# Attention kernel: values and sums of two key tiles in one visit every second step, maxima transposed by VectorE, score banks four and two

## What is computed

```
ada = silu(c) @ Wada + bada
shift_msa, scale_msa, gate_msa, shift_mlp, scale_mlp, gate_mlp = split(ada, 6)
h = _ln(x) * (1 + scale_msa) + shift_msa
q, k, v = (h @ W + b).reshape(B, L, H, DH) for each of the three
A = softmax(scale * einsum('blhe,bshe->bhls', q, k))
out = einsum('bhls,bshd->blhd', A, v)
x = x + gate_msa * (out @ Wo + bo)
m = gelu((_ln(x) * (1 + scale_mlp) + shift_mlp) @ W1 + b1) @ W2 + b2
return x + gate_mlp * m
```

## Time and profile before

| | us |
|---|---|
| median of 3 runs | 2636.14 |
| lowest and highest | 2632.66, 2636.88 |
| span of the profiled execution | 2625.2 |
| of it: up to the first score of head 0 | about 358 |
| heads 0 to 31 | about 358 to 2178 |
| stage 3 | the rest |
| PE busy | 2543.3 (97%) |
| DVE busy | 1841.4 (70%) |
| POOL busy | 1625.0 (62%) |
| ACT busy | 1309.9 (50%) |

### The profile page before, as it was taken

One profiled execution on the slowest core, in us unless ns is written; L12 is line 12 of the kernel. 1 busy time (PEld: TensorE's weight loads), 2 busy tenths in 40 slices (PEclk: granted clock), 3 DMA queues, 4 the chain that ended last, 5 costly groups with the idle time before them and its releaser, 6 DMA issues.

```text
span 2625.2 us, 45742 instructions
## 1 busy us (share of the span) xinstructions
PE 2543.3 (97%) x13208; PEld 1482.7 (56%) x13208; DVE 1841.4 (70%) x2872; ACT 1309.9 (50%) x2429; POOL 1625.0 (62%) x744
## 2 busy tenths in 40 slices
PE   7999899999999999999999999999999979999998
PEld 5788654444444444444444444444444437888887
DVE  5444588887877878778777787778778745555553
ACT  3333245665666656666666665666656642222221
POOL 0000157887888878888878888878888772112120
PEclk9999999999999999999999999999999989999999
DMA  7655631111211112211122111122111001121100
GB/s 263 207 192 167 153 112 49 33 34 39 60 34 33 33 38 56 40 33 33 35 44 56 33 33 35 35 52 46 33 34 33 21 25 53 49 73 71 48 32 32
DMA packets 141459, 163.15 MB, mean 62 GB/s; under 512 B 76048, under 2 KB 92944, under 8 KB 134032
## 3 DMA queue, kind: packets, MB, share of 16 engines
q1 hardware_dynamic: 140480, 159.95, 23.2%
q10 hardware_dynamic: 720, 0.02, 0.0%
HBM read 100.95 MB, written 58.72 MB: 61 GB/s over the span
## 4 chain that ended last, share of the span: by engine, by line
PE 93%; DVE 3%; issue 1%; ACT 1%; DMA 1%; SPq 0%; POOL 0%; ACTq 0%; POOLq 0%; DVEq 0%
PE ps L1113 21%; PE ps L1015 20%; PE ps L1104 19%; PE ps L1127 18%; PE ps L1118 7%; PE ps L1248 7%; DVE part_max L868 1%; PE ps L1024 1%; DVE weights_r L882 1%; PE ps L1059 1%; PE ps L1047 0%; DMA work<-v_rows 0%; DVE work L942 0%; ACT work L670 0%; DMA work<-in_x 0%
## 5 line engine op out<-in xcount | busy, mean ns | idle before, releaser
L538 POOL TENSOR_TENSOR work<-work 128x1024 f32<-128x1024 f32 x640 | 1505.7, 2395 | 296.7 <-PE ps L1118 262.7
L868 DVE TENSOR_REDUCE part_max<-ps 128x1 f32<-128x512 f32 x1984 | 1229.0, 682 | 321.3 <-PE ps L1104 320.7
L670 ACT ACTIVATE work<-ps 128x512 f32<-128x512 f32 x2048 | 1070.9, 602 | 697.3 <-PE ps L1113 697.2
L1113 PE MATMUL ps<-acts_r 97*128 97x512 f32 x2048 | 836.4, 418 | 26.0 <-ACT work L670 14.7
L1104 PE MATMUL ps<-acts_r 96*128 96x512 f32 x1984 | 811.3, 409 | 6.8 <-DVE part_max L868 6.7
L1113 PEld LDWEIGHTS ps<-acts_r 97*128 97x128 f32 x2048 | 383.1, 190 | 396.7 <-ACT work L670 308.4
L1127 PE MATMUL ps<-work 128*32 128x512 f32 x4096 | 545.3, 604 | 0.0
L1104 PEld LDWEIGHTS ps<-acts_r 96*128 96x128 f32 x1984 | 375.6, 189 | 263.0 <-DVE part_max L868 182.4
L1015 PE MATMUL ps<-acts_r,weights_r 128*128 128x512 f32 x1536 | 380.3, 397 | 5.7 <-DVE acts_r L790 5.7
L1015 PEld LDWEIGHTS ps<-acts_r,weights_r 128*128 128x128 f32 x1536 | 291.1, 191 | 69.3 <-issue 6.8
L547 POOL TENSOR_TENSOR work<-work,gate_b 128x512 f32<-128x512 f32 x60 | 84.5, 1439 | 214.3 <-DMA work<-in_x 172.8
(11 more groups left out here) (69 smaller groups left out, 897.5 us busy)
## 6 DMA issues: line engine op xcount, KB each, us to landing
work<-in_x SPq DMA_DIRECT2D x16, 1024.0 KB, 5.4
acts_r<-q_hi SPq DMA_DIRECT2D x64, 256.0 KB, 4.8
acts_r<-k_hi SPq DMA_DIRECT2D x64, 256.0 KB, 6.4
q_hi<-work SPq DMA_DIRECT2D x32, 256.0 KB, 2.6
q_lo<-work SPq DMA_DIRECT2D x32, 256.0 KB, 3.3
k_hi<-work SPq DMA_DIRECT2D x32, 256.0 KB, 2.6
k_lo<-work SPq DMA_DIRECT2D x32, 256.0 KB, 3.2
v_rows<-work SPq DMA_DIRECT2D x32, 256.0 KB, 2.0
```

The lines of the kernel that those rows point to most:

```text
L538: nc.gpsimd.tensor_tensor(psum_acc[:, at], first, prob[:, t % RING, at], ALU.add).then_inc(add_ok, 1)
L670: nc.scalar.activation(prob[:, t % RING, j * CH:(j + 1) * CH], ps[:, A_BANKS + (u + t * NQ + j) % B_BANKS, :], ACT.Exp, scale=SCALE).then_ ...
L868: nc.vector.tensor_reduce(part_max[:, f // NQ, f % NQ:f % NQ + 1], ps[:, (u + f) % A_BANKS, :], AX.X, ALU.max).then_inc(a_max, 1)
L1113: nc.tensor.matmul(ps[:, A_BANKS + (u + t * NQ + j) % B_BANKS, :], ks[u][0:M_ROW + 1, t * P:(t + 1) * P], qs[u][0:M_ROW + 1, j * CH:(j + 1 ...
```

## The change

Six edits, all in stage 2.

1. The groups no longer stand in each step. `BREAKS` puts those of tiles 0, 1 and 2 in step 3, and from step 5 on those of `t-2` and `t-1` in every odd step, each tile's sum behind its values (`use_tile`). Step 1 takes the last tile of the head before and its closing sum. The groups of a head remain 22.
2. The maximum is not transposed by TensorE. `row_max` is widened to 32 columns, VectorE transposes it in blocks of 32x32 into `max_T`, and the row of q is written by four DMAs of 16x32 elements.
3. It is not negated: the row of k holds -1 in the place of 1.
4. PSUM: four banks for the max pass, two for scores.
5. ScalarE takes output and denominators of the head before both after step 1.
6. GpSimd adds tile 13 in the place of 11, TensorE sums 11 in the place of 13. Two slots of the ring change names for stage 3, so that `norm_apply` waits for tile 14 in the place of 13.

```diff
-POOL_TILES = [0, 1, 2, 3, 5, 6, 7, 9, 10, 11, 12]
+POOL_TILES = [0, 1, 2, 3, 5, 6, 7, 9, 10, 12, 13]
...
-STEP_MAX = NT - 2
-A_BANKS, B_BANKS = 3, 3
+BREAKS = {3: (0, 1, 2), **{t: (t - 2, t - 1) for t in range(5, NT, 2)}}
+STEP_LAST = 1
+A_BANKS, B_BANKS = 4, 2
...
+MAX_PIECES = 4
...
-        SLOT_XC1, SLOT_XN3, SLOT_OTF, SLOT_HTF3 = range(RING)
+        SLOT_XC1, SLOT_OTF, SLOT_XN3, SLOT_HTF3 = range(RING)
...
-        row_max = sb("row_max", [P, NT])
-        neg_max = sb("neg_max", [NT, P], F32R)
+        row_max = sb("row_max", [P, DH])
+        max_T = sb("max_T", [P, DH])
...
-                sp.wait_ge(neg_ok, g + 1)
-                sp.dma_start(qs[u][M_ROW:M_ROW + 1, :].bitcast(F32),
-                             neg_max[:].bitcast(F32)).then_inc(neg_in, 16)
+                sp.wait_ge(maxT_ok, g + 1)
+                row = qs[u][M_ROW:M_ROW + 1, :].bitcast(F32).rearrange("o (t q) -> o t q", q=P)
+                for w in range(MAX_PIECES):
+                    sp.dma_start(row[:, :, w * DH:(w + 1) * DH], max_T[w * DH:w * DH + NT, :]).then_inc(maxT_in, 16)
...
-            def row_of_ones(u):
-                nc.gpsimd.memset(ks[u][M_ROW:M_ROW + 1, :].bitcast(F32), 1.0).then_inc(ones_row, 1)
-                pool.wait_ge(ones_row, u + 1)
-            row_of_ones(0)
+            def row_of_minus_ones(u):
+                nc.gpsimd.memset(ks[u][M_ROW:M_ROW + 1, :].bitcast(F32), -1.0).then_inc(minus_row, 1)
+                pool.wait_ge(minus_row, u + 1)
+            row_of_minus_ones(0)
...
-                        nc.scalar.activation(prob[:, t % RING, j * CH:(j + 1) * CH], ps[:, A_BANKS + (u + t * NQ + j) % B_BANKS, :],
+                        nc.scalar.activation(prob[:, t % RING, j * CH:(j + 1) * CH], ps[:, A_BANKS + (t * NQ + j) % B_BANKS, :],
                                              ACT.Exp, scale=SCALE).then_inc(exp_ok, 1)
-                    if prev and t == 0:
+                    if prev and t == STEP_LAST:
                         take_output(g - 1, (u + 2) % NBUF, uses)
-                    if prev and t == 1:
                         take_denominator(g - 1)
...
-                nc.vector.tensor_reduce(row_max[:], part_max[:], AX.X, ALU.max).then_inc(max_ok, 1)
-            def negate_max(g):
-                dve.wait_ge(maxT_mm, g + 1)
                 if not isinstance(g, int) or g:
-                    dve.wait_ge(neg_in, g * 16)
-                nc.vector.tensor_scalar(neg_max[:], ps[0:NT, 0, 0:P], -1.0, None, ALU.mult).then_inc(neg_ok, 1)
+                    dve.wait_ge(maxT_ok, g)
+                else:
+                    dve.wait_ge(zero_ok, 1)
+                nc.vector.tensor_reduce(row_max[:, 0:NT], part_max[:], AX.X, ALU.max).then_inc(max_ok, 1)
+            def transpose_max(g):
+                dve.wait_ge(max_ok, g + 1)
+                if not isinstance(g, int) or g:
+                    dve.wait_ge(maxT_in, g * (16 * MAX_PIECES))
+                nc.vector.transpose(max_T[:], row_max[:]).then_inc(maxT_ok, 1)
...
-                    nc.vector.tensor_reduce(part_max[:, f // NQ, f % NQ:f % NQ + 1], ps[:, (u + f) % A_BANKS, :], AX.X, ALU.max).then_inc(a_max, 1)
+                    nc.vector.tensor_reduce(part_max[:, f // NQ, f % NQ:f % NQ + 1], ps[:, f % A_BANKS, :], AX.X, ALU.max).then_inc(a_max, 1)
                 row_maxima(g)
-                negate_max(g)
+                transpose_max(g)
...
-            def transpose_max(g):
-                pe.wait_ge(max_ok, g + 1)
-                nc.tensor.matmul(ps[0:NT, 0, 0:P], row_max[:], ident[:], start=True, stop=True).then_inc(maxT_mm, 1)
...
-            chunk(NCHUNK - 1, 1, nxt=False, max_after=FILLS_7, max_at=MAX_AT_7)
+            chunk(NCHUNK - 1, 1, nxt=False, max_after=FILLS_7)
             assert next(fills, None) is None
             def max_scores(g, u, f):
                 pe.wait_ge(a_max, g * FILLS + f - A_BANKS + 1)
                 j = f % NQ
-                nc.tensor.matmul(ps[:, (u + f) % A_BANKS, :], qs[u][0:M_ROW, f // NQ * P:(f // NQ + 1) * P],
+                nc.tensor.matmul(ps[:, f % A_BANKS, :], qs[u][0:M_ROW, f // NQ * P:(f // NQ + 1) * P],
                                  ks[u][0:M_ROW, j * CH:(j + 1) * CH], start=True, stop=True).then_inc(a_mm, 1)
             def scores(g, u, t, j):
                 if t == 0 and j == 0:
-                    pe.wait_ge(neg_in, g * 16 + 16)
+                    pe.wait_ge(maxT_in, (g + 1) * (16 * MAX_PIECES))
                 if not isinstance(g, int) or g or t or j >= B_BANKS:
                     pe.wait_ge(exp_ok, START + g * (NT * NQ) + t * NQ + j - B_BANKS + 1)
-                nc.tensor.matmul(ps[:, A_BANKS + (u + t * NQ + j) % B_BANKS, :], ks[u][0:M_ROW + 1, t * P:(t + 1) * P],
+                nc.tensor.matmul(ps[:, A_BANKS + (t * NQ + j) % B_BANKS, :], ks[u][0:M_ROW + 1, t * P:(t + 1) * P],
...
-            def last_values(g, u):
-                values(g, u, NT - 1)
-                if NT - 1 in PE_TILES:
-                    tile_sum(g, NT - 1)
+            def use_tile(g, u, t):
+                values(g, u, t)
+                if t in PE_TILES:
+                    tile_sum(g, t)
...
-                    pe.wait_ge(neg_ok, g + 1)
...
-                    if t == 0 and prev:
-                        last_values(g - 1, (u + 2) % NBUF)
-                    if t == 1 and prev:
+                    if t == STEP_LAST and prev:
+                        use_tile(g - 1, (u + 2) % NBUF, NT - 1)
                         finish_denominators(g - 1)
-                    if t >= 2 and t - 2 in PE_TILES:
-                        tile_sum(g, t - 2)
-                    if t >= 1:
-                        values(g, u, t - 1)
+                    for tile in BREAKS.get(t, ()):
+                        use_tile(g, u, tile)
...
-                    if nxt and t == STEP_MAX:
-                        transpose_max(g + 1)
                 assert next(fills, None) is None
-                if NT - 2 in PE_TILES:
-                    tile_sum(g, NT - 2)
-            pe.wait_ge(ones_row, 1)
+            pe.wait_ge(minus_row, 1)
             pe.wait_ge(v_ok, START + NCHUNK * TT)
             head(0, 0, 1, False, True)
-            pe.wait_ge(ones_row, NBUF)
+            pe.wait_ge(minus_row, NBUF)
```

19 lines of the change are left out of this document (9 added, 10 removed).

## The result

| us | before | after |
|---|---|---|
| median of the runs | 2635.78 | 2783.35 |
| lowest and highest | 2632.66, 2636.88 | 2777.63, 2792.85 |
| ratio, 95% interval | | 1.0572 [1.0547, 1.0598] |
| span of the profiled execution | 2625.2 | 2775.8 |
| up to head 0's first score | 357.5 | 358.05 |

The change makes the kernel 5.5 to 6.0% slower, as forecast in kind, 46 us above the forecast of 2737. That lies inside the range of 2665 to 2795, but above the 2765 that the forecast's own errors were to reach; the range held it because it was drawn to take in rival B, the falling clock.

What follows compares the result with a forecast made beforehand. TensorE was taken to bound looped heads. 30 x 3.45 = 103.5, -7 at loop turns and +4.5 in the last head gave +101 on the span of 2625.2, 2726; with 10.9 to the median, 2737, range 2665 to 2795.

Steps and rivals of the forecast that it cites:

- rival B: TensorE's clock falls in waits around head ends: about 2790 with one fall each head, 2753 each third head; chance 0.11.
- The looped head: Heads 1 to 30: waits for score banks add 7.0 us, breaks and transpose save 3.57, so 3.45 more each.
- the turn of a bank: Two scores in the same PSUM bank start at least 1.19 us apart; four products between them take only 0.94.
- the quarter in each step: First score of steps 1 to 14 comes 0.25 us late for its bank, 3.5 a head.
- The transpose: Dropping TensorE's transpose of the maxima saves 0.51 us in each looped head.
- The reorder window: Skill's rule, not followed: weight loads pulled ahead make some 20 late scores about 0.1 less late, total about 2677.
- The turn of the loop: Every third head: instructions arrive while the first score waits 0.72 for its bank, 10 x 0.7 = 7 us back.
- the row of maxima: Transpose and four DMAs land 4.3 us behind the row maximum (4.1 to 5.15), hidden before the next head's first score.
- Head 0: First head, held by VectorE, whose work is unchanged: 0, between -3 and +3 us.
- The last head and stage 3: Waits in the last head and norm_apply's later start add 4.5 us, between 0 and +8; stage 3 untouched.
- Rival C: The four DMAs of maxima land one after the other, first score 2.8 us late: +84, 2820; chance 0.05.
- Rival A: Score banks don't bind, a turn under 0.98 between max products: faster, 2530 to 2615; chance 0.12.

Runs made afterwards that it cites:

- experiment 4: Changed kernel with both ScalarE copies moved from behind step 1 to behind step 2: 2758.41 us.
- experiment 1: Kernel before with one edit, four banks for the max pass and two for scores: 2763.56 us.
- experiment 2: Changed kernel with three banks for the max pass and three for scores again: 2728.62 us.
- experiment 5: Kernel before with edits 2 and 3 alone (maxima transposed by VectorE, four DMAs, -1 in the row of k): 2636.07 us, ratio 1.0002.
- experiment 6: Changed kernel with the previous head's last-tile groups and closing sum in step 0, both ScalarE copies behind step 2: 2733.09 us.
- experiment 3: Changed kernel with exponentials of heads 1 to 30 over 256 of 512 columns: 2674.43 us.
- experiment 9: Changed kernel with TensorE's loop unrolled to six heads a turn: 2791.72 us.
- 10: Changed kernel with the loops of TensorE and ScalarE unrolled to 15 heads a turn: 2753.40 us, ratio to before 1.0452.
- 11: Changed kernel with three banks each, groups merged only in steps 5, 9, 12 and 15, max products redistributed, last tile in step 0: 2603.24 us, ratio 0.9874.
- 12: Kernel of experiment 11 with TensorE's loop at six heads a turn: 2598.73 us, ratio 0.9864.

## Why the prediction was right or wrong

**The looped head: right.** Forecast 58.6, which is 3.45 more than before; measured 58.73, 3.63 more. Over 30 heads the rows give 108.9 and the forecast 103.5. Its two halves were also right one by one: the turn of a bank is 1.19 or, at the first scores of steps 1, 2, 5, 7, 10 and 11, 1.09, the quarter in each step is there (0.24 at either), step 2's copies cost 0.84 (forecast 0.98, experiment 4), and two banks alone make 59.23 (experiment 1). The 1.09 is just under the 1.1 that the forecast named as a sign of being wrong. It stands where the bank's last score had followed its neighbour back to back: its exponential starts 0.44 behind it, and 0.54 behind a score that itself came late. Three banks are only 1.4 better, though, and still 2.2 worse than before (experiment 2), so the saving of the merged groups was never all to be had.

**The transpose: the sum right, the term wrong.** The 0.51 was TensorE's time, but it stood in a wait for a bank that the kernel before already had, in the one place without max products. The sentence "with no wait in it" on the head before was wrong there: a record that covers a wait looks like work (experiment 5). In the changed kernel my waits for step 14 were counted separately, so the sum survived.

**The reorder window.** The rows after show 1.19 from score to score in a bank, as the row of before did, and that row was the right choice. The page TensorE: Matmul & The Clock Gate of the Trainium skill, Part 2, says that weight loads are pulled ahead of matmuls in flight. It says nothing of a load that itself waits; here such a load starts with its matmul (within 0.01, 0.05 behind the end of the exponential), was not pulled ahead, and the total of 2677, an estimate for the case that it were, didn't come.

**The turn of the loop: the term that failed.** I forecast 7 us back, 0.7 a turn, because the next head's first score waits for its bank anyway. Little of that came: the turn makes that score 0.93 late on average over the nine turns (1.1 in the second profile), against 1.2 in both profiles of before. Why the overlap gave back only 0.1 to 0.3 isn't shown. One candidate is the row of maxima: at the turns its last DMA lands 4.7 to 5.4 behind the first issue and not 3.56, and at three of the nine (16, 25 and 10, the heads that follow) the profile names that DMA as the last thing the first score waited for. That was another of the forecast's own signs of being wrong. And the term left out two things. ScalarE's loop turns at the same place, and two banks put that on TensorE's path (0.93 more). And the stretch that both leave nearly empty brought the clock down, 2.97 more. On top went from 13.1 to 42.8, plus 29.7 in place of minus 7: 36.7 of the 46 us. The bulk is rival B's mechanism, its variant of one fall each third head, and the sign that the forecast named for being wrong, a clock under 1.00 in looped heads, came. I priced that at 1.7 a fall from the earlier trace rows and gave B 0.11. A fall here stays down 6.8 us and costs 3.0, since TensorE is full in it; in experiment 6 one of 3.4 us costs 1.7.

Why this kernel so much more than the one before, whose turns are as long? Experiments 4 and 6 differ only in where the last tile's groups stand: in step 1 nine falls, in step 0 four. Before, step 0 offered a group behind the turn, for which no score bank has to be free, and a third bank to run on, so one gap came alone. Even so the clock fell once in the first profile of before, at its seventh turn (start of head 22), for 3.4 us and 1.5 us of time, which the forecast had overlooked; in the second profile it never did. Before with two banks (experiment 1) fell at two turns. Which turns are hit is open, and it is not the gap alone: the first turn of before and its seventh left TensorE equally empty, and only behind the seventh the clock fell. Stretches of before as above, two around its first turn and two around its seventh:

```profile
590.00:593.40 3.40, 1.83 (x14) 0.45 (x10) 2.02 (x2) 1.08 (x2) 0.29 (x1) 1.00 0.09 23
593.40:596.80 3.40, 3.39 (x22) 1.48 (x23) 1.29 (x2) 1.08 (x2) 0.00 (x0) 1.00 0.31 76
1588.90:1592.30 3.40, 1.83 (x13) 0.57 (x12) 1.86 (x2) 1.08 (x2) 0.09 (x1) 1.00 0.11 29
1592.30:1595.70 3.40, 3.40 (x15) 1.29 (x19) 1.38 (x2) 1.19 (x2) 0.00 (x0) 0.51 0.31 70
```

**Head 0: +7 between the two first profiles, some 3 in the others.** Forecast 0 (between -3 and +3), measured +7.0 between the two first profiles. The kernel before had 76.5 in its second profile, and 77.8 with edits 2 and 3, at the median of before. So the base of 2625.2 was low. The changed kernel's second profile had 80.1, and the five like it 80 to 80.2 (experiments 3, 4, 6, 9 and 10): some 3 more, at the upper bound of the forecast, and its cause is open. This also explains most of my 10.9 between span and median: the time of an execution lies 1.8 above its span (2777.63 against 2775.8), and 7.6 were that short head 0. As the offset was added, two errors cancel in part, by luck: 7.0 too little in the sum, and 10.9 - 7.6 = 3.3 too much behind it.

**The last head and stage 3: right in sum.** Forecast +4.5, measured +4.4. By its parts it wasn't shown: the last head's last score comes 5.9 later behind its first (82.2 against 76.3, and 77.4 in the second profile of before), and what follows is 1.5 shorter, although the change doesn't touch it.

**The row of maxima: right, away from the turns.** 4.0 behind the row maximum, just under the bounds of 4.1 to 5.15; transpose 0.21 for 0.2. Rival C is out there. But the row is hidden only because the first score waits for its bank until later; with three banks it comes on the path, 0.5 to 0.7 a head (experiments 2, 11 and 12). Rival A, which needed a turn under 0.98 between max products, is out by the 1.09 and 1.19 that stand there, and by experiment 3.

The difference to the forecast adds up: heads +5.4, turns +36.7, up to head 1 +7.6, ends -0.1, offset -3.3: 46.3, which is 2783.35 - 2737.

## What to carry to other kernels

Ask of every double buffer between two engines how many instructions of the producer lie between two uses of one buffer, and compare them with the whole turn (write, read, and the start of the next write), not with the reader's own pace: 1.19 here against 0.49 for an exponential and 0.94 for four steps. Merging work saves its switching cost only if the work that it leaves bare doesn't outrun the other engines: eight breaks a head lost with two buffers (58.73) and with three (57.3) against 55.1 with seventeen, and eleven with three buffers won (53.9). A latency that a wait hides comes back when the wait is taken away: look there next, as at the row of maxima here. And count the turns of every engine's loop, not only of the bound one: with shallow buffers they come on the path one after the other, and the hole that they leave can cost more in clock than in time (2.97 against 1.86 a turn here).

## What the hardware showed that I had not expected

- ScalarE's loop turn is no shorter than TensorE's. Its exponential was issued 2.8 us behind the score that it reads, 2.3 later than usual (experiment 9); TensorE's turn showed up to 1.6 of idle time.
- TensorE's clock went to 1.2 GHz behind 3.4 us in which it had been busy for 1.58. At the turns of the kernel before, one gap of 1.0 to 1.6 with groups close behind it, it stayed at 2.4 GHz in 17 of 18 cases over two profiles. Waits of a quarter in nearly each step, all head long, never moved it between two turns, in any of the runs. The Trainium skill's page TensorE: Matmul & The Clock Gate, in its section on psum-queue depth-cycling, says that small idles from cycling through PSUM banks can make the clock swing; here such waits alone never did, and every fall in heads 1 to 30 stands at a turn or the entry of a loop.
- In the run of experiment 9 the falls stood 180.9 us apart ten times over, although the heads behind which they came were 182.5 and 179.2 apart by turns. So the moment isn't set by the kernel's instructions alone. By what else wasn't tried, and so it is open why a given turn is hit.
- A fp32 transpose of 128x32 on VectorE takes 0.20 to 0.21 us; issuing a small DMA about 0.59 (median of 128), up to 1.24.
